# Shift rows loaded by ScalarE's DMAs at two steps of the batch, and no zero rows under the query stack

## What is computed

```python
def _L0_xattn_ref(q, k, v):
    h = 8
    qh = q.reshape(b * h, d // h, m)
    kh = k.reshape(b * h, d // h, -1)
    vh = v.reshape(b * h, c // h, -1)
    qk = jnp.einsum('bdm,bdn->bmn', qh, kh) * scale
    sm = jax.nn.softmax(qk, axis=-1)
    ret = jnp.einsum('bmn,bcn->bcm', sm, vh)
...
def _L0_ffn_ref(x, wg, W, b):
    probs = jax.nn.softmax(xt @ wg, axis=-1)
    idx = jnp.argmax(probs, axis=-1)
    ...
    expert_out = jnp.einsum('nh,eoh->neo', xt, W) + b[None, :, :]
...
x = x + jnp.tanh(g_xattn[0]) * _L0_xattn_ref(_layernorm(x, axis=-1), ctx_2048, ctx_2048)
x = x + jnp.tanh(g_ffn[0]) * _L0_ffn_ref(_layernorm(x, axis=-1), L0_ffn_wg, L0_ffn_W, L0_ffn_b)
```

## Time and profile before

| | |
|---|---|
| median of three runs | 646.61 us |
| the runs | 651.14, 645.61, 646.61 us |
| span of the profiled execution | 645.9 us |
| PE busy | 533.8 us |
| DVE busy | 469.3 us |
| ScalarE busy | 352.5 us |
| POOL busy | 325.5 us |

### The profile page before, as it was taken

One profiled execution on the slowest core, in us unless ns is written; L12 is line 12 of the kernel. 1 busy time (PEld: TensorE's weight loads), 2 busy tenths in 40 slices (PEclk: granted clock), 3 DMA queues, 4 the chain that ended last, 5 costly groups with the idle time before them and its releaser, 6 DMA issues.

```text
span 645.9 us, 10904 instructions
## 1 busy us (share of the span) xinstructions
PE 533.8 (83%) x2584; PEld 179.0 (28%) x2585; DVE 469.3 (73%) x1017; ACT 352.5 (55%) x457; POOL 325.5 (50%) x574
## 2 busy tenths in 40 slices
PE   0077989798978989999988899889999776889994
PEld 0011222222222323323222322323233133444441
DVE  5387888696878979898988989798987636323332
ACT  2112867575766677686766677686666822111110
POOL 5431536282737556474736557474434436343541
PEclk9999999798999999999999999999999978999998
DMA  4734445364647574846657575835462645543320
GB/s 131 189 105 154 116 134 148 102 151 130 131 150 179 148 171 127 195 136 159 141 142 180 145 167 146 184 113 148 104 141 42 179 132 177 117 144 96 102 79 5
DMA packets 35290, 87.80 MB, mean 136 GB/s; under 512 B 10281, under 2 KB 10430, under 8 KB 35104
## 3 DMA queue, kind: packets, MB, share of 16 engines
q1 hardware_dynamic: 26208, 62.27, 39.3%
q0 software_dynamic: 9056, 25.23, 12.1%
HBM read 64.56 MB, written 27.11 MB: 142 GB/s over the span
## 4 chain that ended last, share of the span: by engine, by line
PE 31%; DMA 18%; DVE 17%; issue 11%; POOL 9%; SPq 3%; ACT 1%; POOLq 0%; DVEq 0%
DMA stacks<-shift_parts 13%; DVE neg_max L756 11%; PE ps_scores L1238 10%; PE ps_pv L1130 7%; PE ps_ring L1099 6%; PE ps_scores L1115 4%; DMA table_dram<-token_i,dest_i 2%; SPq L343 2%; DMA prep<-recs_dram,token_cols 2%; PE ps_pv L1147 2%; POOL table_dram L523 2%; POOL prep L463 2%; DVE den L794 1%; ACT probs L672 1%; PE ps_scores L1225 1%
## 5 line engine op out<-in xcount | busy, mean ns | idle before, releaser
L756 DVE TENSOR_REDUCE neg_max<-ps_ring 128x1 f32<-128x512 f32 x512 | 335.4, 680 | 76.1 <-PE ps_ring L1099 74.1
L672 ACT ACTIVATE probs<-ps_scores 128x1024 f32<-128x1024 f32 x256 | 249.2, 1022 | 112.0 <-PE ps_scores L1115 110.8
L1099 PE MATMUL ps_ring<-stacks 128*128 128x512 bf16 x512 | 201.0, 403 | 55.3 <-DMA stacks<-zeros 30.7
L1115 PE MATMUL ps_scores<-stacks 128*128 128x512 bf16 x512 | 156.1, 388 | 20.2 <-DMA stacks<-shift_parts 19.2
L1130 PE MATMUL ps_pv<-probs,v_ones 128*32 128x512 f32 x1024 | 138.2, 612 | 0.0
L1099 PEld LDWEIGHTS ps_ring<-stacks 128*128 128x128 bf16 x512 | 49.6, 97 | 240.6 <-DVE neg_max L756 191.0
L1238 PE MATMUL ps_scores<-w_sb,probs 128*128 x184 | 87.2, 619 | 3.3 <-DVE v_ones L927 1.3
L435 POOL TENSOR_SCALAR rs<-mv 128x1 f32<-128x1 f32 x32 | 6.1, 189 | 131.7 <-DVE mv L772 89.4
L1115 PEld LDWEIGHTS ps_scores<-stacks 128*128 128x128 bf16 x512 | 48.1, 101 | 65.4 <-issue 25.2
L710 ACT COPY probs<-ps_scores 128x512 f32<-128x512 f32 x23 | 13.4, 587 | 82.2 <-PE ps_scores L1225 82.2
L927 DVE TENSOR_TENSOR v_ones<-ps_scores,stacks 128x512 f32<-128x512 f32 x23 | 15.9, 692 | 57.6 <-PE ps_scores L1238 55.2
(11 more groups left out here) (138 smaller groups left out, 481.1 us busy)
## 6 DMA issues: line engine op xcount, KB each, us to landing
parts_dram<-prep POOLq DMA_DIRECT2D x16, 768.0 KB, 7.1
stacks<-parts_dram SPq DMA_DIRECT2D x64, 192.0 KB
recs_dram<-rec SPq DMA_DIRECT2D x16, 514.0 KB, 3.9
stacks<-parts_dram SPq DMA_DIRECT2D x64, 128.0 KB
w_sb<-w_t SPq DMA_DIRECT2D x16, 512.0 KB, 9.4
prep<-x_perm SPq DMA_DIRECT2D x16, 256.0 KB, 5.2
prep<-k_perm SPq DMA_DIRECT2D x16, 256.0 KB, 8.3
v_in<-v_t SPq DMA_DIRECT2D x16, 256.0 KB, 8.9
```

Source lines behind the costliest of these rows:

```text
L672: nc.scalar.activation(probs[:, k % 2, 2 * jp:2 * jp + 2], ps_scores[:, jp], ACT.Exp).then_inc(exp_done, 1)
L756: nc.vector.tensor_reduce(neg_max[:, g, j, c:c + 1], ps_ring[:, u.slot(n)], AX.X, ALU.max, negate=True).then_inc(ring_free, 1)
L1099: nc.tensor.matmul(ps_ring[:, u.slot(n + c)], q_stack[0:KA, B.p, g, j, c * 128:(c + 1) * 128], k_stack[0:KA, B.p, g, j], start=True, stop= ...
L1115: last = nc.tensor.matmul(ps_scores[:, jp, j % 2], k_stack[0:KA, B.p, g, j, c * 128:(c + 1) * 128], q_stack[0:KA, B.p, g, j], start=True, ...
```

## The change

Four edits:

- `load_shift` moves from SP to ScalarE. For batch 0, group 0 it stands ahead of the first exponentials; for group 1 of the batch at step 2, behind the exponentials and the casts of that step; for group 0 of the next batch at step 6, behind the exponentials.
- The tile of zeros, its memset and the DMA of zeros in `load_stack` go; a stack has six DMAs.
- The matmuls of `scores_for_max` contract over 96 partitions (KS) instead of 128 (KA); those of `scores` still over 128.
- The wait for the pads (`pads_in`) moves from SP's first stack to PE's `scores` in batches 0 and 1.

```diff
-        zeros = sb("zeros", [NP, NJ * DM], BF16)
...
-        STACK_CONSTS, VALUE_CONSTS = 3, 4
-        DVE_CONSTS = 17
+        STACK_CONSTS, VALUE_CONSTS = 2, 3
+        DVE_CONSTS = 16
...
-                if B.known(0) and g == 0:
-                    sp.wait_ge(pads_in, 16)
-                sp.dma_start(q_stack[KS:KS + NP, B.p, g].rearrange("p j m -> p (j m)"),
-                             zeros[:]).then_inc(stack_in[B.p][g], 16)
-
-            def load_shift(B, g):
-                sp.wait_ge(shift_ready, B.b * 2 + (g + 1))
-                for t in range(NP):
-                    sp.dma_start(q_stack[KS + t:KS + t + 1, B.p, g].rearrange("o j (c m) -> o (j c) m", c=NC),
-                                 shift_parts[:, g, t]).then_inc(shift_in[g], 16)
...
-            load_shift(Batch(0, 0), 0)
             sp.wait_ge(pool_const, POOL_CONSTS)
...
                 load_weights(B)
-                load_shift(B, 1)
...
                     load_rows_keys(B.plus(4))
-                if nxt:
-                    load_shift(B.plus(1), 0)
                 if stack:
                     load_stack(B.plus(2), 1)
...
+            def load_shift(B, g):
+                act.wait_ge(shift_ready, B.b * 2 + (g + 1))
+                for t in range(NP):
+                    nc.scalar.dma_start(q_stack[KS + t:KS + t + 1, B.p, g].rearrange("o j (c m) -> o (j c) m", c=NC),
+                                 shift_parts[:, g, t]).then_inc(shift_in[g], 16)
+
...
+            load_shift(Batch(0, 0), 0)
             act.wait_ge(dve_const, DVE_CONSTS)
...
+                    if k == 2:
+                        load_shift(B, 1)
                     if k == 5:
                         read_low(B)
+                    if k == 6 and nxt:
+                        load_shift(B.plus(1), 0)
...
-                           lambda: nc.vector.memset(zeros[:], 0.0),
...
-                    pe.wait_ge(stack_in[B.p][g], B.i * (16 * 7) + 16 * 7)
+                    pe.wait_ge(stack_in[B.p][g], B.i * (16 * 6) + 16 * 6)
                 for c in chunks:
                     wait(pe, ring_free, u.free(n + c))
-                    nc.tensor.matmul(ps_ring[:, u.slot(n + c)], q_stack[0:KA, B.p, g, j, c * 128:(c + 1) * 128],
-                                     k_stack[0:KA, B.p, g, j], start=True, stop=True).then_inc(ring_full, 1)
+                    nc.tensor.matmul(ps_ring[:, u.slot(n + c)], q_stack[0:KS, B.p, g, j, c * 128:(c + 1) * 128],
+                                     k_stack[0:KS, B.p, g, j], start=True, stop=True).then_inc(ring_full, 1)
...
                     pe.wait_ge(shift_in[g], B.b * 48 + 48)
+                    if B.known(0) or B.known(1):
+                        pe.wait_ge(pads_in, 16)
```

## The result

The kernel after takes 652.87 us (median of 20 runs, 647.78 to 665.82) against 645.66 (median of 20, 640.86 to 651.25): ratio 1.0096, 95% interval 1.0065 to 1.0128. The ratio is of the quicker executions of both; the medians over all 20 stand at 1.011. The prediction said 628.2, in 620 to 639.

The account below looks back on a forecast made before the run. PE's waits for late shift rows at step 0, 17.1 us in 11 waits, were to go: 24.35 us off, 3.9 + 2.0 on, span 645.9 to 627.5, median 628.2 us; range 622 to 639, the forecast itself 620 to 634.

Parts of the forecast that it names:

- Past the backlog, the third lands after 2.3.: Step 6, group 0: issued by ScalarE, the third shift DMA lands at +27.3, needed at +28.04, so the stall goes.
- 17.1 + 2.1 + 2.95 us: Savings: PE's waits at step 0 of batches 2 to 12, its first-batch wait, and time lost to clock falls.
- rival B: ScalarE's queue leads past nothing; group 0's shift rows land when the backlog has drained, as now: 648 us, chance 0.08.
- The page's rule: Skill page: all issuers' DMAs share 16 engines (648 us), against SP and ACT rings taking turns (628 us).
- Batch 0: 2.1: First batch: PE's 2.07 us wait for shift rows behind the stacks all goes.
- Step 2: 3.9: Group 1: three issues delay ScalarE, so scores come late; 0.3 us lost in each of 13 batches, 3.9 in all.
- rival C: ScalarE's issues are dear and step 2 becomes the stall: 668 us, mild form 641; chance 0.05, mild form 0.02 of it.
- The stack's rest: 2.0: Step 0: part of the three 3 us stalls remains as waiting for the stack; 2 us taken, of 0 to 9.
- rival A: The stack's late landing takes the stall's place at step 0: 636 us, chance 0.12.
- The clock: 2.95: Batches 2 and 3: TensorE's clock falls behind 3 us standstills, costing 2.0 and 0.95 us, go with the stalls.
- 96 rows: nothing: Maxima's matmuls over 96 rows instead of 128: taken as no change, since DVE's maxima set steps 0 to 4.
- Last batch: 1.5: End: the bias load goes earlier and frees the scatter, 0 to 2.4 us to gain; 1.5 taken.

Follow-up runs that it names:

- best_sp: Kernel after with split query-stack loads, scatter in the next batch, batch 15's group 1 shift rows early, but SP issuing shift rows: 612.89 us, 0.953.
- even_after: Kernel after with each broadcast load of the query stack split into separate DMAs of 16 partitions, one per copy: 621.02 us, ratio 0.957.
- zeros_only: Kernel after with shift rows issued by SP again at the old places; only zero rows, their DMAs and 128-row contraction gone: 649.79 us, 0.9998.

## Why the prediction was wrong, step by step

- **"Past the backlog, the third lands after 2.3."** This is the step that failed, and 17.1 + 2.1 + 2.95 us hung on it. The wait was not for SP's queue: on a queue of ScalarE's own most packets went at once, but a DMA has landed only with its last one. In batches 2 to 12 the third landed after 4.7 to 7.8 us, and the waits came to 20.1 us instead of none. It was rival B, to which I gave 0.08, though I wrote its evidence down myself: the keys show the engines busy until 267.07. I set against it group 1's quick landings "while loads are under way", without asking which loads: those fly when the broadcast loads and the scatter are over.
- **The page's rule.** I set two sections of the Trainium skill side by side, one giving 648 and one the sum's 628, and took the second. "Issuing engines are not separate DMA queues" (page "DMA: Bandwidth & Descriptors") was right, and best_sp shows it at its plainest. The turns between rings did not help three DMAs of which six packets waited five us.
- **Batch 0: 2.1.** Won 0.3, for the same reason: the rows land behind the first stacks. Splitting the loads won 7.9 there. The memset's 0.7 did not show either.
- **Step 2: 3.9, and ScalarE's issue price.** I took SP's 0.62 as time of ScalarE. It is 0.51 to 0.61 in the queue for most, beside a running activation, and no time of ScalarE's own shows for it in the kernel after. The lower bound was the right one, and rival C had no ground there; that a slow issue can hold ScalarE is seen once, in even_after (last section).
- **The stack's rest: 2.0, rival A.** No wait for a stack showed. The stacks were the backlog, but not late themselves.
- **The clock: 2.95.** The falls of batches 2 and 3 went, others came in the slices at 194 to 210 and 226 to 242 us, beside stalls of 2.3 and 3.5 us; nothing was won.
- **96 rows: nothing.** Not far off for the matmuls: 0 to 1% by the two pairs above, not settled. But without the zero DMA the keys stand 1 us nearer to the scatter, and the move's 1.3% gain became a loss. I had cost that DMA by SP's idle time alone, and never asked what the transfers behind it would meet. The runs show that the loss is there only with both the scatter and the backlog in place. How 1 us decides so much, and why the same nearness cost zeros_only nothing, they do not show.
- **Last batch: 1.5.** The part behind batch 12 won 3.4. The scatter was freed of the bias as said; the price was 4.75, not 2 to 4, and its cause not the bias but the scatter itself. The end's larger gain hides part of the loop's loss of 4.7 in the span.
- **What would show it wrong:** "landings of 5 us on ScalarE's queue (B)". That is what the trace shows. B's 648 is also the nearest of the prices to 652.87, though by luck in part: it holds 3.9 us for step 2, which cost nothing, and nothing for the missing zero DMA.

## What to carry to other kernels

When a small transfer lands late behind big ones, do not look first at who issues it, but at how the big ones are spread over the DMA engines: in place of leading broadcasts of two and three copies one DMA per copy was worth 4% here, where in the end the issuer was worth nothing. Count how many packets of the small one begin late. Here some did where the backlog held them, and none did where the landing was late by the scatter. A scatter of single numbers to DRAM was in flight for 7 to 9 us in the kernel before and held what should land beside it; give it a place where nobody waits. Before moving or dropping a small DMA ask what the ones behind it will then meet.

## What the runs showed of the hardware that was not expected

- DMAs that ScalarE issues (0.51 to 0.61 us each) run beside its activations; now and then they take longer, and then they do hold ScalarE: two in even_after took 3.28 us from 239.03, and step 7's exponentials began at 242.50, 0.2 us behind their end, though PE had finished their scores at 240.8. The shift rows were late by it too, and PE stood 2.60 us for them at 246.65.
- Of the 48 packets of three small DMAs, six began five us after the other 42 while the broadcast loads were in flight; with the loads split none did.
- A scatter of 512 bytes, issued 0.5 us earlier, put off the landing of another queue's 4 KB DMA to 6.9 us (2.1 at most for the three of group 0 before it), with next to nothing else in flight. The 16 increments of its semaphore followed the scatter's one for one, each 0.16 to 0.21 us behind.
- Taking one DMA of 12 KB out of each stack, in a queue that moves 61 MB in the whole run, made the kernel with ScalarE's issues 2 to 3% slower, and 0.2% when the scatter stood elsewhere; with SP's issues (zeros_only, 0.9998) it made no difference.
